# Expert results turned and shared out one step sooner, relational groups routed in pairs, and half of the values ahead of the scores

## The chip, the cores and the metric

The kernel runs on one core of one Trainium2 chip. The metric is the device time of one execution in microseconds (us). Five engines work side by side, each through its own list of instructions: TensorE (PE), VectorE (DVE), ScalarE (ACT), GpSimd (POOL) and SyncE (SP, whose part here is to issue transfers). They wait for one another by semaphores.

## The reference

The input x has 128 graphs of 64 nodes with 128 features, 8192 tokens in all. Four layers follow each other, each added to its input after a layer norm:

```
x = x + gnn0(layernorm(x), adj)       # 3 rounds: aggregate over adj, then a GRU cell
x = x + ffn0(layernorm(x))            # 8 experts, top 2 of 8 by gate score
x = x + gnn1(layernorm(x), nodemask, adj)   # relational graph conv
x = x + ffn1(layernorm(x))            # 8 experts, top 2, own layer norm, gelu

# an expert layer
scores = x @ Wg + bg;  top 2 experts of each token, weights p
h = relu(x @ W1[e] + b1[e])           # 128 -> 512   (gelu in the second)
y = h @ W2[e] + b2[e]                 # 512 -> 128
out = sum over the two experts of p[e] * y

# the relational layer, one direction
h = x @ W.T;  g = h @ Wg.T
vals = (h + b) * sigmoid(g + bg);  out = relu(sum over neighbours of vals)
```

## The kernel before, in words

Tokens lie in 64 tiles of 128, in 16 groups of four tiles. The stages follow one another: an opening (to about 106 us), the gated graph layer (to about 478), the first expert stage (to about 804), the relational layer (806 to 1066), the second expert stage (to about 1386) and the combine, which gathers each token's two results and writes the output. A value is kept as two 16-bit parts, hi and lo, so a product is three matmuls (the helper `passes`, L205 to L207). No scheduler is at work: every engine's order is the order of the calls in its own function, written by hand.

**An expert stage** (`experts`). Tokens have been sorted by expert into rows of the DRAM buffer `slots`, and are worked through in 36 blocks: 24 full blocks of 512 rows, and 12 blocks that are pairs of halves of 256 rows with an expert each. Buffers go round in rings of RING = 3. In its step b each engine does this:

- TensorE: for each quarter c of the hidden layer, `up_c(b + 1, c)` and `down_c(b, c)`, three matmuls each for a full block, twice as many of half the width for a pair. Then `turn(b - 1)`: four transposes (L1547) of the result that VectorE has put in `yT`, into the PSUM bank `YB`.
- ScalarE: for each quarter, the activation (L1586) and the hi part (L1592) of block b + 1.
- VectorE: `collect(b - 1)` (L1630), which takes the result of down out of PSUM, adds the bias and lets turn go; every third step `addresses` (L1617 to L1623), which works out rows and shares for three blocks; `share_out(b - 2)` (L1639), which multiplies the turned result by its tokens' weights; then four `lo` (L1605), the lo parts of block b + 1.
- GpSimd: four scatters (L1511) of block b to the DRAM buffer `results`, behind share_out.
- SyncE: the transposing load of block b + 3 (L1461), then the tags of block b + 2 (L1471), and in some steps a `tail` (L1477).

`rounds` writes the first steps out, puts a loop of six steps over the middle, and writes the last ones out.

**The relational stage** (`relational`). Group g passes through steps g to g + 4 and beyond. In step s TensorE turns group s - 1 (`turn_a`, L1861) and group s - 4 (`turn_b`, L1925), then computes the gate scores of group s - 4 (`scores`, L205 to L207 with WGATE and `xT_b`), the relational values of group s - 1 (`values`, four tiles in two PSUM halves v = 0 and 1; biases L1877, then products with WREL and `xT_a`) and the sums over neighbours of group s - 2 (L1890). A half of values waits until VectorE has taken the values before it out of the same PSUM half (`val_sb`).

VectorE's step: the mixture of the group's two expert results (L1674), lo parts, norms, values of group s - 2 (L2069, two halves), scores of group s - 4 (L2141, L2145), shifts (L2054 to L2064), `v_los` (L2091), and, when `chosen_at(s)` says so, the choice of two experts for one or two groups (L581 to L600, some lines further on the sorting). GpSimd computes the power for the norms (`root`, L1804) and sends finished rows of `ROWS` to `slots` by indirect transfers (L644); `relational_sends` says how many in which step. ScalarE turns PSUM copies into `xT_a` and `xT_b` (`turned_a`, `turned_b`, L2006) and, in the first SPLIT = 6 steps, scales by the norms itself (`norms_a`).

## Time and profile before

| what | value |
|---|---|
| median of 3 runs | 1425.64 us (1419.89 to 1427.88) |
| profiled execution, its own time | 1428.36 us |
| its span in the profile | 1426.6 us |
| mean granted TensorE clock, as a share of full speed | 0.787 |
| busy: PE / DVE / ACT / POOL | 918.1 / 905.9 / 765.8 / 733.9 us |

The span is what the profiler saw of the profiled execution; 1.76 us of that execution's time lie around it. Busy time counts an engine's own work and not its waits, branches or semaphores. A mean over the span mixes stages with different limits, so the stages are read one by one.

### The profile page before, as it was taken

To read this page: it belongs to the slowest core of one execution; us is meant where nothing else is said; L and a number is where in the kernel's file an instruction comes from. 1 tells how busy PE (TensorE), PEld (TensorE's weight loads), DVE (VectorE), ACT (ScalarE), POOL (GpSimd) and SP (SyncE) were. 2 spreads that over 40 slices of the span, in tenths; PEclk is the share of its full clock that TensorE was granted. 3 is DMA by queue.
4 is the path that set the end of the run, shared out by engine and by line. 5 is a ranking of instruction groups with operands and counts; after the bars stand their busy time and mean duration, and the time that the engine had idled before them with its cause. 6 is when DMAs were issued, how large, how long until landed. Compare 5 with 4: busy or idle time off the path is not lost. (4 is left out here: it accounts for less than half of the span.)

```text
span 1426.6 us, 23103 instructions
## 1 busy us (share of the span) xinstructions
PE 918.1 (64%) x5850; PEld 519.1 (36%) x5851; DVE 905.9 (64%) x2456; ACT 765.8 (54%) x1392; POOL 733.9 (51%) x717
## 2 busy tenths in 40 slices
PE   2368778888862357888787176656432968888820
PEld 1244344444432123434565133323210433346620
DVE  5967799999985345555544367767642645554626
ACT  2476767677762145666565165656431655666710
POOL 3501132876757646556544416567566444655540
PEclk9579999999995679899988555555556998999955
DMA  9233221221201524424221223321131342333209
GB/s 249 90 127 94 77 46 23 59 61 48 59 22 42 136 58 100 91 67 85 64 50 45 71 90 119 104 65 55 32 62 52 87 105 58 84 67 70 61 28 340
DMA packets 199164, 115.62 MB, mean 81 GB/s; under 512 B 155084, under 2 KB 175710, under 8 KB 198528
## 3 DMA queue, kind: packets, MB, share of 16 engines
q1 hardware_dynamic: 169008, 69.54, 20.8%
q0 software_dynamic: 17408, 34.13, 7.4%
q10 hardware_dynamic: 12624, 10.49, 2.8%
q8 instruction: 54, 0.88, 0.3%
q14 instruction: 70, 0.57, 0.1%
HBM read 43.80 MB, written 51.61 MB: 67 GB/s over the span
## 5 line engine op out<-in xcount | busy, mean ns | idle before, releaser
L644 POOL DMA_INDIRECT slots<-ROWS,pos x256 | 265.4, 1037 | 78.5 <-issue 71.4
L1511 POOL DMA_INDIRECT results<-e1ys,e1home x144 | 155.5, 1080 | 136.1 <-DVE e1ys L1639 93.7
L1511 POOL DMA_INDIRECT results<-e2ys,e2home x144 | 151.1, 1049 | 136.2 <-DVE e2ys L1639 93.0
L1586 ACT ACTIVATE e1hf<-psum,VT 128x512 f32<-128x512 f32 (+1 forms) x192 | 104.3, 583 | 151.6 <-PE psum L207 82.0
L1605 DVE SCALAR_TENSOR_TENSOR e1hs<-e1hf,e1hs 128x512 f16<-128x512 f32 x144 | 95.6, 690 | 127.4 <-ACT e1hs L1592 88.9
L1586 ACT ACTIVATE e2hf<-psum,VT 128x512 f32<-128x512 f32 (+1 forms) x192 | 104.8, 582 | 126.0 <-remote 59.1
L1605 DVE SCALAR_TENSOR_TENSOR e2hs<-e2hf,e2hs 128x512 f16<-128x512 f32 x144 | 95.8, 691 | 112.5 <-ACT e2hs L1592 83.0
L1363 POOL TENSOR_TENSOR a_Z<-a_Z,a_H 128x512 f32<-128x512 f32 x48 | 68.2, 1420 | 161.5 <-ACT a_Z L1093 159.2
L205 PE MATMUL psum<-e2hs,W 128*128 128x512 f16 (+1 forms) x192 | 66.7, 347 | 55.9 <-DVE e2hs L1605 25.9
L205 PE MATMUL psum<-a_hT,WHH 128*128 128x512 f16 x144 | 58.8, 408 | 52.5 <-ACT a_Z L1093 48.3
L205 PE MATMUL psum<-e1xT,W 128*128 128x512 f16 (+1 forms) x192 | 67.6, 352 | 38.5 <-DMA e1xT<-slots 16.7
L205 PE MATMUL psum<-e1hs,W 128*128 128x512 f16 (+1 forms) x192 | 67.4, 351 | 35.8 <-DVE e1hs L1605 24.9
L1592 ACT ACTIVATE e1hs<-e1hf 128x512 f16<-128x512 f32 x144 | 86.9, 631 | 0.0
L1592 ACT ACTIVATE e2hs<-e2hf 128x512 f16<-128x512 f32 x144 | 86.7, 631 | 0.0
L205 PE MATMUL psum<-e2xT,W 128*128 128x512 f16 (+1 forms) x192 | 66.7, 348 | 23.4 <-issue 11.0
L1804 POOL TENSOR_TENSOR c_rs<-c_var,mhalf 128x12 f32<-128x12 f32 (+2 forms) x22 | 40.5, 1843 | 79.9 <-DVE c_var L2082 45.1
L207 PE MATMUL psum<-e1xT,W 128*128 128x512 f16 (+1 forms) x192 | 67.7, 353 | 3.3 <-issue 3.2
L206 PE MATMUL psum<-e1hs,W 128*128 128x512 f16 (+1 forms) x192 | 67.5, 352 | 2.7 <-issue 1.7
L206 PE MATMUL psum<-e1xT,W 128*128 128x512 f16 (+1 forms) x192 | 67.5, 351 | 2.7 <-issue 2.7
L207 PE MATMUL psum<-e1hs,W 128*128 128x512 f16 (+1 forms) x192 | 67.4, 351 | 2.7 <-issue 2.5
L207 PE MATMUL psum<-e2xT,W 128*128 128x512 f16 (+1 forms) x192 | 66.5, 346 | 1.6 <-issue 1.5
L206 PE MATMUL psum<-e2xT,W 128*128 128x512 f16 (+1 forms) x192 | 66.5, 346 | 0.4 <-issue 0.4
(363 smaller groups left out, 2643.6 us busy)
## 6 DMA issues: line engine op xcount, KB each, us to landing
c_G<-results SPq DMA_DIRECT2D x32, 256.0 KB
d_G<-results SPq DMA_DIRECT2D x32, 256.0 KB, 5.2
slots<-slots SPq DMA_DIRECT2D x16, 264.0 KB
W<-in_L_ffn_W_dram SPq DMA_DIRECT2D x16, 256.0 KB, 3.4
kept<-a_cut SPq DMA_DIRECT2D x16, 256.0 KB, 2.6
slots<-ROWS,pos POOLq DMA_INDIRECT x256
W<-kept SPq DMA_DIRECT2D x8, 512.0 KB
out_dram<-X ACTq DMA_DIRECT2D x16, 256.0 KB, 7.1
```

The lines of the kernel that those rows point to most:

```text
L205: pe.matmul(out, lhs(0), rhs(0), start=start, stop=False, skip_group_check=True)
L206: pe.matmul(out, lhs(0), rhs(1), start=False, stop=False, skip_group_check=True)
L207: return pe.matmul(out, lhs(1), rhs(0), start=False, stop=stop, skip_group_check=True)
L644: pool.indirect_dma_start(out=slots, out_offset=bass.IndirectOffsetOnAxis(ap=k["pos"][:, c, t:t + 1], axis=0), in_=k["ROWS32"][:, t, :], i ...
L1363: pool.tensor_tensor(Z[p % 2][:, :], Z[p % 2][:, :], H[p][:, :], ALU.mult).then_inc(zh_sb, 1)
L1511: pool.indirect_dma_start(out=k["results"][m], out_offset=bass.IndirectOffsetOnAxis(ap=home[:, GT * b + q:GT * b + q + 1], axis=0), in_=ys ...
L1586: t = act.activation(hf[c][:, cols], HB[c][:, cols], func, bias=VT[:, bass.ds(e * CH + b1_col + c, 1)], scale=1 / PS)
L1592: act.activation(hs[j][:, 0, c, :], hf[c][:, :], ACT.Copy, scale=AS).then_inc(h_hi, 1)
L1605: dve.scalar_tensor_tensor(out=hs[j][:, 1, c, :], in0=hf[c][:, :], scalar=AS, in1=hs[j][:, 0, c, :], op0=ALU.mult, op1=ALU.subtract).then_ ...
L1804: pool.tensor_tensor(rstd[s % 4][:, lo:hi], var[s % 2][:, lo:hi], k["mhalf"][:, lo:hi], ALU.pow)\
```

## The change

The diff does three things. In the experts TensorE's turn of block b - 1 moves from the end of step b to behind its second quarter, VectorE shares out block b - 1 in step b instead of b - 2 (behind its second lo), the addresses are worked out one step earlier, and SyncE reads the tags ahead of the next load. In the relational stage the choice of experts is made for pairs of groups from the first on (the first two groups were chosen one by one), with the sends of GpSimd one step later and eight at once. And TensorE's values are split in two halves, the first of which stands ahead of the scores; ScalarE's `turned_b` stands ahead of `norms_a` where both are in a step.

```diff
--- before.py
+++ after.py
@@ -1488,6 +1488,8 @@
                     sp.wait_ge(counted, 1)
                 if RING <= b < RING + E:
                     tail(b - RING)
+                if 1 <= b and b + 2 < NBLK:
+                    read_tags(b + 2, rows.pop(b + 2))
                 if b + RING == EARLY:
                     sp.wait_ge(listed, 1)
                     sp.wait_ge(tails, 16 * E)
@@ -1495,8 +1497,6 @@
                 if b + RING < NBLK:
                     sp.wait_ge(h_ps, 4 * b + 4)
                     rows[b + RING] = load(b + RING)
-                if 1 <= b and b + 2 < NBLK:
-                    read_tags(b + 2, rows.pop(b + 2))
 
         @block.gpsimd
         def _(pool):
@@ -1568,8 +1568,8 @@
                         known[:] = [e, who(b + 2)]
                     elif c == 1:
                         known[:] = [e, None]
-                if not isinstance(b, int) or b:
-                    turn(b - 1, 1 - v)
+                    if c == 1 and (not isinstance(b, int) or b):
+                        turn(b - 1, 1 - v)
             rounds(pe, step)
             turn(NBLK - 1, (NBLK - 1) % 2)
 
@@ -1647,13 +1647,13 @@
             def step(b, j, i, v):
                 if not isinstance(b, int) or b:
                     collect(b - 1, 1 - v)
-                if j == RING - 1:
+                if j == 1:
                     addresses(b - j, i)
-                if not isinstance(b, int) or b > 1:
-                    share_out(b - 2, (j - 2) % RING, i - (j < 2), v)
                 for c in range(CH):
                     if not last(b):
                         lo(b + 1, (j + 1) % RING, c)
+                    if c == 1 and (not isinstance(b, int) or b):
+                        share_out(b - 1, (j - 1) % RING, i - (j < 1), 1 - v)
                 if m == 0 and isinstance(b, int) and b == RING - 1:
                     for h in range(2):
                         half = slice(h * NODES, (h + 1) * NODES)
@@ -1661,8 +1661,7 @@
             rounds(dve, step)
             end = NBLK - 1
             collect(end, end % 2)
-            for b in (end - 1, end):
-                share_out(b, b % RING, b // RING, b % 2)
+            share_out(end, end % RING, end // RING, end % 2)
 
 
 
@@ -1681,16 +1680,16 @@
         sp.dma_start(G[:, c, :, :], rows[:, c, bass.ds(GT * g, GT), :]).then_inc(sem, 16)
 
 
-BATCHES = [(0, 1), (1, 1)] + [(g, 2) for g in range(2, 16, 2)]
+BATCHES = [(g, 2) for g in range(0, 16, 2)]
 ROUTED = 4
 SPLIT = 6
 
 
 def relational_sends(NG):
 
-    first = ROUTED + 1
+    first = ROUTED + 2
     n = NG + ROUTED + 1
-    wanted = [0 if s < first else (8, 6, 2)[s - first] if s < first + 3 else 8 if s < NG else CARRY for s in range(n)]
+    wanted = [0 if s < first else 8 if s < NG else CARRY for s in range(n)]
     early = 2 * GT * (NG - QUAD)
     return [max(min(w, early - sum(wanted[0:s])), 0) for s, w in enumerate(wanted)]
 
@@ -1865,11 +1864,10 @@
                 pe.wait_ge(lo_a, g + 1)
                 turn_over(TAh, tok_a[p]).then_inc(a_ps, 1)
 
-            def values(g, p):
+            def values(g, p, v):
 
                 pe.wait_ge(a_sb, g + 1)
-                for q in range(GT):
-                    v = q // 2
+                for q in range(2 * v, 2 * v + 2):
                     if q % 2 == 0:
                         wait_from(pe, val_sb, 2 * g + v - 1)
                     o = Vv[v][:, q % 2, :, :].rearrange("p s d -> p (s d)")
@@ -1939,10 +1937,12 @@
                     turn_a(s - 1, (s - 1) % 2)
                 if 0 <= s - 4 < NG:
                     turn_b(s - 4)
+                if 0 <= s - 1 < NG:
+                    values(s - 1, (s - 1) % 2, 0)
                 if 0 <= s - 4 < NG:
                     scores(s - 4)
                 if 0 <= s - 1 < NG:
-                    values(s - 1, (s - 1) % 2)
+                    values(s - 1, (s - 1) % 2, 1)
                 if 0 <= s - 2 < NG:
                     neighbours(s - 2, s % 2)
                 b, g, n = chosen_at(s)
@@ -2008,10 +2008,10 @@
             def step(s):
                 if 0 <= s - 1 < NG:
                     turned_a(s - 1, (s - 1) % 2)
+                if 0 <= s - 4 < NG:
+                    turned_b(s - 4)
                 if s < SPLIT:
                     norms_a(s, s % 2)
-                if 0 <= s - 4 < NG:
-                    turned_b(s - 4)
                 if 0 <= s - 2 < NG:
                     v_his(s - 2, s % 2)
                 if SPLIT <= s < NG:
```

How the order of the instructions changes is shown at three places, with the line numbers of each version. The first is VectorE's list from collect on, for one full block in the first expert stage, without the last lo (e1yT is the collected result, e1ys the shared out one, e1hs the lo parts). Before:

```order
L1630 TENSOR_SCALAR e1yT<-psum,VT 128x512
L54 ISA
L1637 REGISTER_ALU
L1639 ISA
L1639 TENSOR_TENSOR e1ys<-psum,e1share 128x512
L1604 ISA
L1605 SCALAR_TENSOR_TENSOR e1hs<-e1hf,e1hs 128x512
L1604 REGISTER_ALU
L1605 SCALAR_TENSOR_TENSOR e1hs<-e1hf,e1hs 128x512
L1604 REGISTER_ALU
L1605 SCALAR_TENSOR_TENSOR e1hs<-e1hf,e1hs 128x512
```

After the change:

```order
L1630 TENSOR_SCALAR e1yT<-psum,VT 128x512
L1604 ISA
L1605 SCALAR_TENSOR_TENSOR e1hs<-e1hf,e1hs 128x512
L1604 REGISTER_ALU
L1605 SCALAR_TENSOR_TENSOR e1hs<-e1hf,e1hs 128x512
L54 ISA
L1637 REGISTER_ALU
L1639 ISA
L1639 TENSOR_TENSOR e1ys<-psum,e1share 128x512
L1604 REGISTER_ALU
L1605 SCALAR_TENSOR_TENSOR e1hs<-e1hf,e1hs 128x512
```

The sharing out moved from between collect and the four lo parts to behind the second of these, and it belongs to a block one later than it did.

The second place is TensorE's list in the last step of the first expert stage (e1hs times W are down's matmuls, e1yT turned by identf are the transposes). Before, the last down matmuls and what follows them:

```order
L205 REGISTER_ALU
L205 MATMUL psum<-e1hs,W 128x256
L206 MATMUL psum<-e1hs,W 128x256
L207 REGISTER_ALU
L207 MATMUL psum<-e1hs,W 128x256
L1547 MATMUL psum<-identf,e1yT 128x128 x8
L152 UNCONDITIONAL_BRANCH
```

After the change, the middle of the last block's matmuls:

```order
L205 REGISTER_ALU
L205 MATMUL psum<-e1hs,W 128x256
L206 MATMUL psum<-e1hs,W 128x256
L207 REGISTER_ALU
L207 MATMUL psum<-e1hs,W 128x256
L1547 MATMUL psum<-identf,e1yT 128x128 x4
L205 REGISTER_ALU
L205 MATMUL psum<-e1hs,W 128x256
```

Before, both the last two blocks' transposes stood at the very end (x8). Now those of the last but one stand behind half of the last block's matmuls, and four are left at the end.

The third place is TensorE's list in the fifth step of the relational stage (ident turns tokens and rows, WGATE are scores, relbias and WREL are values). Before, the dots standing for six more rows of scores in the same pattern:

```order
L1861 MATMUL psum<-ident,c_tok_a 128x128 x8
L1925 MATMUL psum<-ident,ROWS 128x128 x8
L205 MATMUL psum<-WGATE,c_xT_b 128x8
L206 MATMUL psum<-WGATE,c_xT_b 128x8
L207 MATMUL psum<-WGATE,c_xT_b 128x8
...
L205 MATMUL psum<-WGATE,c_xT_b 128x8
L206 MATMUL psum<-WGATE,c_xT_b 128x8
L207 MATMUL psum<-WGATE,c_xT_b 128x8
L1877 MATMUL psum<-relbias,ones 128x256 x2
L205 MATMUL psum<-WREL,c_xT_a 128x256
L206 MATMUL psum<-WREL,c_xT_a 128x256
L207 MATMUL psum<-WREL,c_xT_a 128x256
```

After the change:

```order
L1860 MATMUL psum<-ident,c_tok_a 128x128 x8
L1923 MATMUL psum<-ident,ROWS 128x128 x8
L1875 MATMUL psum<-relbias,ones 128x256 x2
L205 MATMUL psum<-WREL,c_xT_a 128x256
L206 MATMUL psum<-WREL,c_xT_a 128x256
L207 MATMUL psum<-WREL,c_xT_a 128x256
L1875 MATMUL psum<-relbias,ones 128x256 x2
L205 MATMUL psum<-WREL,c_xT_a 128x256
L206 MATMUL psum<-WREL,c_xT_a 128x256
L207 MATMUL psum<-WREL,c_xT_a 128x256
L205 MATMUL psum<-WGATE,c_xT_b 128x8
L206 MATMUL psum<-WGATE,c_xT_b 128x8
```

The scores' twelve matmuls moved behind the first two of the four tiles of values.

## Rows read from the trace of the kernel before

**Rows 1.** The page, part 1: busy us (share of the span) and instructions

```profile
PE 918.1 (64%) x5850; PEld 519.1 (36%) x5851; DVE 905.9 (64%) x2456; ACT 765.8 (54%) x1392; POOL 733.9 (51%) x717
```

**Rows 2.** Windows: stretch, length, busy per engine (instructions), granted clock, DMA share, GB/s

```profile
535.70:667.70 132.00, 110.84 (x505) 50.77 (x506) 76.48 (x135) 82.42 (x143) 76.62 (x72) 0.94 0.40 85
...
806.00:1066.00 260.00, 141.96 (x993) 77.56 (x994) 171.94 (x794) 134.07 (x276) 148.11 (x164) 0.51 0.26 79
1120.60:1252.30 131.70, 106.63 (x477) 48.11 (x476) 70.60 (x126) 80.14 (x139) 70.93 (x68) 0.91 0.36 83
```

**Rows 3.** Waits of ScalarE, 500 to 800 us: total, times, longest

```profile
ACT e1hf L1586 <- remote: 57.3, 13, 11.6
ACT e1hf L1586 <- PE psum L207: 54.2, 31, 8.8
```

**Rows 4.** Timeline of TensorE and VectorE: start, us, instruction, [idle before <-releaser]

```profile
566.20 0.38 PE L205 MATMUL psum<-e1hs,W 128*128 128x512 f16 x1 [2.88 <-DVE e1hs L1605]
...
566.78 0.63 PE L207 MATMUL psum<-e1hs,W 128*128 128x512 f16 x1
...
1156.60 0.60 PE L1547 MATMUL psum<-identf,e2yT 128*128 128x128 f32 x4
1157.04 0.38 PE L205 MATMUL psum<-e2xT,W 128*128 128x512 f16 x1
...
1159.62 0.38 PE L205 MATMUL psum<-e2xT,W 128*128 128x512 f16 x1
...
1162.21 0.60 PE L1547 MATMUL psum<-identf,e2yT 128*128 128x128 f32 x4
...
1158.91 0.75 DVE L1630 TENSOR_SCALAR e2yT<-psum,VT 128x512 f32<-128x512 f32 x1
...
1307.37 0.27 PE L205 MATMUL psum<-e2xT,W 128*128 128x256 f16 x1 [1.19 <-issue]
```

**Rows 5.** Timeline of GpSimd and VectorE at the expert stages' ends

```profile
789.11 0.98 POOL L1511 DMA_INDIRECT results<-e1ys,e1home  x1 [7.76 <-DVE e1ys L1639]
...
803.28 0.98 POOL L1511 DMA_INDIRECT results<-e1ys,e1home  x1 [0.30 <-issue]
...
1384.92 0.98 POOL L1511 DMA_INDIRECT results<-e2ys,e2home  x1 [0.31 <-issue]
...
780.51 0.69 DVE L1605 SCALAR_TENSOR_TENSOR e1hs<-e1hf,e1hs 128x512 f16<-128x512 f32 x1 [4.26 <-ACT e1hs L1592]
...
786.13 0.88 DVE L1630 TENSOR_SCALAR e1yT<-psum,VT 128x256 f32<-128x256 f32 x2 [0.69 <-issue]
...
787.65 0.69 DVE L1639 TENSOR_TENSOR e1ys<-psum,e1share 128x512 f32<-128x512 f32 x1
```

**Rows 6.** Timeline of VectorE in the relational stage, 847 to 855 us

```profile
847.71 0.74 DVE L2069 SCALAR_TENSOR_TENSOR c_sg<-psum,c_sg 128x256 f32<-128x256 f32 x2
...
850.97 0.18 DVE L581 TENSOR_REDUCE v_top<-S 128x4 f32<-128x32 f32 x1
...
853.50 0.19 DVE L600 TENSOR_TENSOR v_both<-v_wide 128x32 f16<-128x32 f32 x1
854.36 1.42 DVE L1674 TENSOR_TENSOR X<-X,c_G 128x512 f32<-128x512 f32 x2 [0.66 <-issue]
```

**Rows 7.** Timeline of TensorE at the same place

```profile
849.25 0.19 PE L205 MATMUL psum<-WGATE,c_xT_b 128*128 128x8 f16 x1 [2.56 <-ACT c_xT_b L2006]
...
849.66 0.60 PE L1877 MATMUL psum<-relbias,ones 1*128 1x256 f16 x2
...
852.24 0.60 PE L1877 MATMUL psum<-relbias,ones 1*128 1x256 f16 x2
```

**Rows 8.** Relational stage, VectorE, 868 to 1010 us: its waits, its score additions

```profile
DVE S L2141 <- PE psum L207: 15.9, 7, 3.3
DVE c_shift_a L2054 <- POOL c_rs L1804: 4.5, 3, 1.5
...
868.00:1010.00 142.00, 1.88 (x10) 0.51 0.26 80
```

## The prediction

> **What bounds the kernel now.** I began with the page's line of busy time [rows 1]: no engine passes 64% of the 1426.6 us, so no single engine is the bound. The stages were then set side by side by busy time in windows [rows 2]. The opening, the gated graph and the combine are untouched by the diff and are left out. What is left is the first expert stage, the relational stage (806 to 1066 us) and the second expert stage.
>
> The two expert stages run 24 full blocks and then 12 pairs of halves. Between their third and twenty-first turn lie 132.0 and 131.7 us, which is 18 steps of 7.33 us. TensorE works 107 to 111 us of each such stretch [rows 2], and where nothing disturbs it a step takes 5.62 us, from turn to turn [rows 4]. The difference is not spread evenly. The chain of waits of ScalarE [rows 3] puts 57.3 us in only 13 waits that nothing local ends, and 54.2 us in 31 waits for TensorE, the longest 8.8 us. What stops the loop for 3 to 8 us every few steps is not shown by a row that I found; a step between two stops is bound by TensorE.
>
> The relational stage is different. VectorE is busy 171.9 of 260.0 us and TensorE 142.0 at a granted clock of 0.51 [rows 2], the lower of its two levels (1.2 GHz). VectorE works through a fixed list, and its largest wait there is for the scores: 15.9 us in 7 waits over ten steps [rows 8]. So here VectorE's list, and what it waits for, is the time.
>
> **Part 1, the end of each expert stage: −9 us.** Before, block 33's products were scaled (share_out) only after the last step, so GpSimd stood idle 7.76 us and then issued twelve scatters in a row, from 789.11 to 803.28 + 0.98 [rows 5], 1.29 us each. Moved one step earlier, share_out(33) stands behind a lo of 780.51 [rows 5], and its four scatters fall into that idle time. Eight are left. Four scatters less are 4 × 1.29 = 5.1 us. They begin behind share_out(34), which needs collect(34), ended 786.13 + 0.88 = 787.01 [rows 5], a turn of 0.60 [rows 4] and a share of 0.69: about 788.3, against share_out(33)'s end at 787.65 + 0.69 = 788.34 now. So nearly nothing of the 5.1 is lost to the start. The turn now stands in front of half of the last block's down matmuls and holds them for about 1 us; block 35's scatters have four of 1.29 us in front of them as cover. I charge 0.5 us. The second expert stage ends with the same twelve, the last at 1384.92 [rows 5]. 2 × (5.1 − 0.5) = −9.2 us, and the relational stage and the combine wait for these ends.
>
> **Part 2, the middle of each expert step: 0, between −40 and +37 us.** VectorE's work is reordered and TensorE's four transposes move from a place where their input had long been ready to one where it is hardly ready. In the undisturbed step collect ends at 1158.91 + 0.75 = 1159.66, while the matmul in front of which the transposes now stand starts at 1159.62 [rows 4]: 0.04 us late. A second amount comes on top. Collect waits in VectorE's list for the last lo, and so for up's last piece of the step before. Between that piece and the place where collect is now needed, the transposes used to stand with 1157.04 − 1156.60 = 0.44 us [rows 4], and they don't any more. The loop from TensorE over ScalarE and VectorE back to TensorE so closes 0.04 + 0.44 = 0.48 us late, and the shortest step is 5.62 + 0.48 = 6.10 us. A step takes 7.33 on the mean, 1.2 us more than that; if the stops stay and take the wait into themselves, the price is 0. If each step pays it: 24 × 0.48 = 11.5 us, and for the 12 half blocks, whose collect takes 0.88 [rows 5], about 0.6 us each by the same loop, 7 us: 2 × 18.5 = 37 us over both experts. The other way, if a short wait in each step keeps the long stops from building up, a step could come down to some 6.5 us (0.4 above the shortest, my choice): 24 × 0.83 × 2 = −40 us. I take 0, since [rows 3] puts most of the loss in waits far longer than 0.48 us (57.3 / 13 = 4.4 us each in the first row). VectorE has the same instructions as before; the addresses come one step earlier behind tags that are read at the end of the step before, and the queue of SP waits for them once in three steps as it did. I cost both at nothing: loads are issued more than a step before use.
>
> The clock could make a wait dearer than its length. Behind an idle of 2.88 us the matmuls go from 0.38 to 0.63 us each [rows 4], the lower level of TensorE's clock. A wait of 1.19 us is followed by a matmul of half a block in 0.27 us [rows 4], which is the upper level. So a wait of 0.5 us should cost its own length. The Trainium skill ("TensorE: Matmul & The Clock Gate", section "Loop structure matters more than you think") says that the loop nest decides whether matmuls stay warm, and names a long wait between matmuls as the bad form. By that rule, if it held for the new waits, a step whose matmuls all ran at the lower level would pay 24 × 0.25 = 6 us on top of the wait; the trace shows such a fall only behind long stops, so the sum goes by the trace.
>
> **Part 3, pairs of groups in the relational stage: −2 us.** The first choice of experts for a single group falls away. It fills VectorE from 850.97 to 853.50 + 0.18 in the fifth step, and the next step's first instruction starts at 854.36 after 0.66 of issue [rows 6]: 2.7 us and some of the issue, −2.9 us. The choice for two groups at once then costs more than the one for a single group, since its operations grow from 32 to 64 columns (I choose a fifth, +0.5 us), and the placing moves one step behind: +0.2. GpSimd's first sends come one step later and eight at once; the same number is sent by the end, and its root of 2.30 us may be some 1 to 2 us later in one step, beside the choice. Sum −2.2 us, ends −3 and +1.
>
> **Part 4, values in front of scores: +10 us, between 0 and +15.** TensorE now computes the first half of values before the scores. In step 4 VectorE frees the first half of the values about 0.4 us after 847.71 [rows 6]; the scores' matmuls stood from 849.25, behind a wait of 2.56 us for ScalarE's turned copy [rows 7]. One half of values is 852.24 − 849.66 = 2.58 us at this clock [rows 7]. It fills TensorE's wait, but it cannot start before VectorE's own values, so the scores reach VectorE some 2.75 us behind these in every step, where VectorE has nothing else in its list. Ten steps of that are 27.5 us against the 15.9 it waits there now [rows 8]: +11.6, and for the 13 steps with this pattern +15. Three of the ten steps already lose 1.5 us waiting for GpSimd's root right behind [rows 8], 4.5 us that the later scores absorb: 15 − 4.5 = +10.5. The lower end, 0, is that waits elsewhere in the list (88 us of the stage are idle on VectorE, [rows 2]) take it all, or that a busier TensorE is granted its higher clock and the half takes 1.3 us. I take +10, near the rows. ScalarE's turned_b ahead of norms in two steps is nothing: the values are in front of its reader now.
>
> **Sum.** −9.2 + 0 − 2.2 + 10 = −1.4 us, on the profiled execution's own time of 1428.36: 1427.0 us. The median of the runs is 2.7 us under that execution, so 1424.3 in its terms; I say 1425.
>
> **The rivals.**
> - *Likeliest (0.45): the stops absorb the reordering.* 1418 to 1433, with −9 from the ends and about +8 from the scores.
> - *The turn becomes the bound (0.23).* Place: TensorE at the transposes in the middle of an expert step, held for collect. It decides from a quarter of its price on: 9 us turn "same" into slower; in full 37, or 1462. For it speaks that collect already ends 0.04 us after it will be needed [rows 4]. Against it, the 1.2 us that a mean step has above the shortest. This is the case on the slower side.
> - *A shorter loop (0.17).* Share_out one step sooner frees buffers and the long stops shrink: −10 to −40, so 1385 to 1415. For it, the 57.3 us of waits without a local cause [rows 3]; against it, the diff touches nothing that I can tie to them.
> - *The scores come no later (0.15).* The first half of values fits into TensorE's 2.56 us of wait [rows 7] and costs 0 to 3 us: 1415 to 1418.
> - *The waits in front of the turn cool TensorE (0.03, inside the 0.23).* Its matmuls then take 0.63 instead of 0.38 us for part of a step. Eight full steps of the 48 are enough for 8 × 6 = 48 us: 1473. Against it, the wait of 1.19 us that left the clock up [rows 4]. The Trainium skill's rule of the loop nest, cited above, speaks for this one.
>
> **How the numbers follow.** About 0.5% (7 us: below 1418.5, above 1432.8) is what a measurement of this kernel can tell from no change. Faster: 0.10 of the likeliest case, 0.15 of the shorter loop, 0.13 of the scores' case = 0.38. Slower: 0.08 + 0.20 = 0.28. Same: 0.34. The range of 8 in 10 reaches half into the two wide cases: 1403 to 1450; the likeliest case alone gives 1418 to 1433.
>
> **What would show it.** In the new profile: eight scatters behind each other at either expert's end, and GpSimd's idle time before them shorter; undisturbed expert steps of 6.1 instead of 5.62 us, with a short wait of TensorE for VectorE's collect in front of the transposes; the stretch of 18 steps still near 132 us; VectorE's wait for scores near 27 us in ten relational steps, and the stage near 266 us; no choice in its fifth step. The prediction is wrong if the long stops of the expert loop change in number or length, since I could name no cause for them, or if the waits for scores don't grow.

## The result and the profile after

The changed kernel took 1442.62 us in the median of 17 runs (1431.73 to 1447.49), the kernel before beside it 1430.11 us (1409.90 to 1453.73): a ratio of 1.0128, with a 95% interval of 1.0091 to 1.0164, so the change is slower. The ratio leaves out the executions of the kernel before that took over 1.5% longer than its fastest; the two medians as they stand give 1.0087. The profiled execution took 1443.63 us with a span of 1441.5, 14.9 us more than before's.

The windows of the changed kernel (columns as in [rows 2]) show where these lie. The first two are the 18 steps between the third and twenty-first turn of either expert stage, the last reaches from the first mixture of the relational stage to the first product of the second experts:

```profile
540.80:670.60 129.80, 110.51 (x505) 50.24 (x505) 74.73 (x132) 84.68 (x144) 78.23 (x71) 0.97 0.37 85
1140.50:1270.50 130.00, 110.17 (x504) 50.28 (x504) 74.32 (x132) 83.52 (x142) 79.18 (x73) 0.96 0.39 88
807.40:1080.10 272.70, 139.28 (x985) 78.40 (x986) 168.34 (x774) 132.29 (x272) 142.51 (x123) 0.50 0.23 70
```

and the same relational stretch of the kernel before:

```profile
810.10:1063.00 252.90, 138.96 (x986) 76.49 (x987) 171.01 (x793) 132.64 (x274) 144.76 (x122) 0.51 0.25 77
```

In the first expert stage 18 steps are 2.2 us shorter than before. For the second stage the row of [rows 2] can't be used: it has 477 matmuls where 18 steps have 505, so it covers 17 steps. All 18 of the kernel before lie in

```profile
1120.60:1258.20 137.60, 112.48 (x506) 50.90 (x505) 75.62 (x134) 85.09 (x147) 74.91 (x72) 0.91 0.37 84
```

which is 7.6 us more than after the change. The relational stretch is 19.8 us longer, with hardly more work in it (0.3 us on TensorE, 1.9 on its weight loads, less on the others): it is waiting. All that lies outside it gives back 4.9 us, 2.7 ahead of it and 2.2 behind it, which makes the 14.9. VectorE's score additions say which wait it is. These are the changed kernel's, all 16 of the stage, with the idle time in front of them:

```profile
L2141 DVE TENSOR_TENSOR S<-psum,c_rs x16: 181/192/193, 848.5 to 1069.0; 128x32 f32<-128x32 f32 x16
...
  PE psum L207: 42.3, 15
```

and these the kernel before's:

```profile
L2141 DVE TENSOR_TENSOR S<-psum,c_rs x16: 179/191/192, 849.8 to 1052.4; 128x32 f32<-128x32 f32 x16
...
  PE psum L207: 21.7, 11
```

20.6 us more in this one wait. Within a step of the changed kernel (timeline of VectorE, then TensorE; ten of the 13 steps have this wait of 2.77 us, three a longer one) one sees the chain:

```profile
906.20 0.75 DVE L2069 SCALAR_TENSOR_TENSOR c_sg<-psum,c_sg 128x256 f32<-128x256 f32 x2
909.72 0.19 DVE L2141 TENSOR_TENSOR S<-psum,c_rs 128x32 f32<-128x32 f32 x1 [2.77 <-PE psum L207]
...
906.77 0.58 PE L1875 MATMUL psum<-relbias,ones 1*128 1x256 f16 x2 [1.58 <-DVE c_sg L2069]
...
909.18 0.21 PE L205 MATMUL psum<-WGATE,c_xT_b 128*128 128x8 f16 x1
```

VectorE frees the first half of the values, TensorE has idled 1.58 us for that, computes 2.4 us of values at the lower clock, then the scores; VectorE stands still for 2.77 us.

At the end of the first expert stage the scatters look so (timeline of GpSimd, then of VectorE; ten scatters of the same pitch lie between the first two rows):

```profile
784.97 1.33 POOL L1511 DMA_INDIRECT results<-e1ys,e1home  x1 [4.24 <-DVE e1ys L1639]
...
799.48 0.98 POOL L1511 DMA_INDIRECT results<-e1ys,e1home  x1 [0.30 <-issue]
...
783.51 0.68 DVE L1639 TENSOR_TENSOR e1ys<-psum,e1share 128x512 f32<-128x512 f32 x1
...
786.13 0.88 DVE L1630 TENSOR_SCALAR e1yT<-psum,VT 128x256 f32<-128x256 f32 x2 [0.68 <-issue]
```

There are still twelve scatters in a row, but they begin ahead of the collect of block 34 (786.13) and not behind it. From the start of that collect to the end of the last scatter it is 14.3 us; before, it was 18.1 (786.13 to 804.26, [rows 5]). In the second stage it is 13.1 us instead of 18.1. So the two ends are 3.8 and 5.0 us shorter, and all the rest outside the relational stretch is 3.9 us longer in these two executions.

The long stops of the expert loop changed their form. ScalarE's waits from 500 to 800 us that nothing local ends were 13 with 57.3 us [rows 3]; they are now fewer, while its waits for TensorE grew from 54.2 to 71.3:

```profile
ACT e1hf L1586 <- PE psum L207: 71.3, 46, 7.0
ACT e1hf L1586 <- remote: 24.0, 4, 10.1
```

### The profile page after: what moved, and what is told of

The parts are those of the page before. It is cut to its first block and busy times, and to the rows that moved or that the text cites. A ratio compares the mean times of both kernels' runs of the same rounds, so it can differ in the third digit from the quotient of the medians.

```text
span 1441.5 us, 23094 instructions
## 1 busy us (share of the span) xinstructions
PE 915.9 (64%) x5849; PEld 523.1 (36%) x5850; DVE 902.1 (63%) x2437; ACT 768.9 (53%) x1390; POOL 739.9 (51%) x717
## 3 DMA queue, kind: packets, MB, share of 16 engines
q0 software_dynamic: 17408, 34.13, 7.3%
## 5 line engine op out<-in xcount | busy, mean ns | idle before, releaser
L1511 POOL DMA_INDIRECT results<-e1ys,e1home x144 | 158.7, 1102 | 129.2 <-DVE e1ys L1639 87.3
L1511 POOL DMA_INDIRECT results<-e2ys,e2home x144 | 155.6, 1081 | 130.3 <-DVE e2ys L1639 87.8
L205 PE MATMUL psum<-e1hs,W 128*128 128x512 f16 (+1 forms) x192 | 66.2, 345 | 10.3 <-DVE e1hs L1605 9.8
L207 PE MATMUL psum<-e1hs,W 128*128 128x512 f16 (+1 forms) x192 | 65.5, 341 | 0.7 <-issue 0.7
L206 PE MATMUL psum<-e1hs,W 128*128 128x512 f16 (+1 forms) x192 | 65.8, 343 | 0.0
```

The lines of the kernel that those rows point to most:

```text
L205: pe.matmul(out, lhs(0), rhs(0), start=start, stop=False, skip_group_check=True)
L206: pe.matmul(out, lhs(0), rhs(1), start=False, stop=False, skip_group_check=True)
L207: return pe.matmul(out, lhs(1), rhs(0), start=False, stop=stop, skip_group_check=True)
L1511: pool.indirect_dma_start(out=k["results"][m], out_offset=bass.IndirectOffsetOnAxis(ap=home[:, GT * b + q:GT * b + q + 1], axis=0), in_=ys ...
```

## The experiments

Each kernel was timed in rounds with the kernel before on the same chip. **The chips differ.** On the chip of the first four, the kernel before took 1227.7 us; on the others 1418 to 1432 us. A ratio therefore only speaks for its kind of chip.

**The parts alone, on the chip where the kernel before takes 1227.7 us.** First, the changed kernel with the split undone:

```diff
+                if 0 <= s - 4 < NG:
+                    scores(s - 4)
                 if 0 <= s - 1 < NG:
                     values(s - 1, (s - 1) % 2, 0)
-                if 0 <= s - 4 < NG:
-                    scores(s - 4)
-                if 0 <= s - 1 < NG:
                     values(s - 1, (s - 1) % 2, 1)
```

> The changed kernel with one part undone: TensorE computes the scores ahead of both halves of the values again; experts, pairs and ScalarE's order stay changed. Theory 1 (the first half of the values keeps VectorE waiting for the scores): the stretch from the first to the last mixture of the relational stage falls from 200.9 us to 183 or less (before: 183.3), VectorE's waits for the scores in the steps 4 to 16 fall from 39 to about 19 us, and the kernel takes about 18 us less than the changed one: near 1.000 of the kernel before, or 0.5% under it if the shorter ends of the experts count. Theory 2 (the later and larger sends and choices of the pairs cost the time): the stretch stays near 200 us and the ratio near 1.013.

Second, the reverse, the kernel before with only that split:

> The kernel before with one part alone: the first half of the values ahead of the scores on TensorE. Theory 1: the relational stage grows by 18 to 21 us, ratio 1.013 to 1.015. Theory 2: by 0 to 5 us, ratio under 1.004. The expert stages are those of before.

Third, the kernel before with only the expert part (SyncE's, TensorE's and VectorE's edits of `experts` in the diff above):

> The kernel before with the expert part alone (turn, share out, addresses and tags one step sooner). By the profiles, each expert stage ends with 8 scatters in a row instead of 12, and the steps in the middle cost nothing on balance: ratio 0.994 to 1.000. If the turn in the middle of the step is a bound that the one profile hid, ratio 1.005 to 1.02, with undisturbed steps of 6.1 us instead of 5.62.

Fourth, only BATCHES and `relational_sends`:

> The kernel before with the pairs alone (choices for two groups from the first on, sends from step 6 on, eight at once). Theory 1: one choice less, minus 2 to 3 us from the first to the last mixture, ratio 0.997 to 1.000. Theory 2: the stretch grows by 5 us or more.

| run | ratio | interval | relational stretch, us | wait for scores, us |
|---|---|---|---|---|
| r1_no_split | 1.0434 | 1.0419 to 1.0448 | 235.4 | 3.3 |
| r2_split_only | 1.0120 | 1.0101 to 1.0139 | 250.4 | 39.3 |
| r3_experts_only | 1.0437 | 1.0420 to 1.0455 | 236.4 | 5.8 |
| r4_pairs_only | 1.0002 | 0.9990 to 1.0014 | 235.6 | 6.3 |

Theory 1 holds in kind: the split alone makes the relational stretch 14.0 us longer than with the experts' part alone (250.4 against 236.4), and it alone brings the wait for the scores. The cost is less than the 18 to 21 us expected, because another wait shrinks: 33.5 us more are spent on the scores than in r3 (39.3 against 5.8), and the wait for GpSimd's root right behind them falls from 20.5 to 3.9 us. These are VectorE's waits for the root in r3 and then in r2:

```profile
DVE c_shift_a L2053 <- POOL c_rs L1803: 20.5, 13, 3.2
```

```profile
DVE c_shift_a L2055 <- POOL c_rs L1804: 3.9, 4, 1.2
```

The pairs are worth nothing that can be measured; theory 2 falls. But the expert part, which looked free in the profile after, costs 54 us here. The windows of 18 expert steps, r4 and then r3:

```profile
511.80:613.00 101.20, 101.20 (x505) 50.67 (x505) 77.83 (x135) 85.39 (x142) 79.13 (x72) 1.00 0.55 112
```

```profile
511.40:627.10 115.70, 107.39 (x505) 49.88 (x505) 74.34 (x132) 85.27 (x144) 85.61 (x76) 0.98 0.44 98
```

Without the expert part a full step takes 5.62 us all the time: here the fastest step of [rows 4] is the only one, and TensorE is never idle in this window. With it, the mean is 6.43 us: most steps take 6.20 from turn to turn, a few up to 8.6. The half blocks behind them pay more, 7.05 us a step against 5.68 in most steps of r4. The ends are shorter here too: from the collect of block 34 to the end of the last scatter 14.4 and 14.3 us in r3, 18.9 and 19.5 in r4. So the middle of the steps costs the 54 us and the 9.7 that the ends give back, some 64 us. The waits of TensorE in the window, its timeline in r3, then VectorE's and two rows of ScalarE's:

```profile
PE psum L1547 <- DVE e1yT L1630: 12.7, 19, 5.0
```

```profile
551.64 0.65 PE L1547 MATMUL psum<-identf,e1yT 128*128 128x128 f32 x4 [0.55 <-DVE e1yT L1630]
...
557.96 0.66 PE L1547 MATMUL psum<-identf,e1yT 128*128 128x128 f32 x4 [0.49 <-DVE e1yT L1630]
...
555.00 0.68 DVE L1639 TENSOR_TENSOR e1ys<-psum,e1share 128x512 f32<-128x512 f32 x1
555.61 1.29 DVE L1605 SCALAR_TENSOR_TENSOR e1hs<-e1hf,e1hs 128x512 f16<-128x512 f32 x2
557.16 0.75 DVE L1630 TENSOR_SCALAR e1yT<-psum,VT 128x512 f32<-128x512 f32 x1 [0.25 <-issue]
...
554.37 0.69 ACT L1586 ACTIVATE e1hf<-psum,VT 128x512 f32<-128x512 f32 x1
554.96 1.14 ACT L1592 ACTIVATE e1hs<-e1hf 128x512 f16<-128x512 f32 x2
```

TensorE waits at every turn for collect, and collect stands behind the last two lo parts. The share_out of 555.00 in front of these delays them little: the last lo needs ScalarE's last hi part, which ends at 554.96 + 1.14 = 556.10, and it takes 0.69 us itself, so it could not end before 556.79; it ends at 555.61 + 1.29 = 556.90. In a half block the same wait is longer, and 0.68 us of issue stand in front of collect (r3, TensorE, then VectorE):

```profile
660.11 0.66 PE L1547 MATMUL psum<-identf,e1yT 128*128 128x128 f32 x4 [1.15 <-DVE e1yT L1630]
...
659.18 0.88 DVE L1630 TENSOR_SCALAR e1yT<-psum,VT 128x256 f32<-128x256 f32 x2 [0.68 <-issue]
```

**The expert part in variants, where the kernel before takes 1431 us.** The changed kernel again; the expert part alone with the turn and share_out at `c == 2` instead of `c == 1`; with the turn at `c == 1` and share_out at `c == 3`; and the kernel before with the pairs, with addresses and tags one step sooner as in the change, and with turn and share_out moved in the last step only (`if c == 1 and last(b)`):

```diff
-                    if c == 1 and (not isinstance(b, int) or b):
+                    if c == 2 and (not isinstance(b, int) or b):
                         turn(b - 1, 1 - v)
...
-                    if c == 1 and (not isinstance(b, int) or b):
+                    if c == 2 and (not isinstance(b, int) or b):
                         share_out(b - 1, (j - 1) % RING, i - (j < 1), 1 - v)
```

(the first variant, against the expert part of the change; the second has `c == 3` in the second place only; the third, against the kernel before, TensorE's part of it:)

```diff
+                    if c == 1 and last(b):
+                        turn(b - 1, 1 - v)
-                if not isinstance(b, int) or b:
+                if (not isinstance(b, int) or b) and not last(b):
                     turn(b - 1, 1 - v)
```

> The changed kernel itself, again beside the kernel before. If the chip is like that of the first experiments (expert steps of 5.6 us without long stops in the kernel before, which took 1227.7 us there), the experts' part costs 52 to 55 us and the values' part 14 to 16 us, and the ratio is 1.053 to 1.057. If it is like that of the first measurement (1430 us for the kernel before, long stops), the ratio is 1.010 to 1.016.

> The expert part alone, but turn and share_out stand behind the third quarter (c == 2) instead of the second. Theory A (TensorE is held at turn for collect, which comes too late there): a quarter later collect is 1.3 us early, TensorE no longer waits, the steps come back to 5.6 to 5.8 us and the ratio is 0.99 to 1.005. Theory B (VectorE's share_out between the lo parts holds ScalarE and with it the next products): the ratio stays at 1.03 or above.

> The expert part alone, the turn behind the second quarter as in the change, but share_out behind the last lo part instead of the second. Theory A: collect is even later by 0.69 us, since it stands behind share_out, and the ratio rises above 1.044, to some 1.06. Theory B: ScalarE is freed and the ratio falls to 1.01 to 1.02.

> The kernel before with the pairs and, of the expert part, only its end: addresses and tags one step sooner as in the change, but turn and share_out move only in the last step, so that the steps in the middle keep their order. If the shorter end is worth what the trace says and the middle is what costs, the ratio is 0.992 to 0.998; if the moved tags or addresses cost something, 1.002 or above.

| run | ratio | interval | 18 steps in its profile, us |
|---|---|---|---|
| s3_changed | 1.0098 | 1.0062 to 1.0133 | 130.7 |
| s1_turn_later | 1.0174 | 1.0119 to 1.0229 | 143.0 |
| s2_share_last | 1.0042 | 1.0004 to 1.0080 | 122.9 |
| s6_tail_pairs | 1.0010 | 0.9920 to 1.0099 | 143.0 |

The kernel before spread from 1399 to 1456 us beside these four, so small differences between the ratios mean little; the plain medians give 1.0061, 1.0061, 0.9991 and 0.9958. Theories A and B had been made for a chip without stops and say little here: 18 steps take 123 to 143 us against the 101 of the other chip, whatever the order. Neither is borne out: A expected s1 below 1.005 and s2 at 1.06, B had s1 at 1.03. None of these orders was run on a chip without stops, so what each would be worth there stays open. The shorter end alone (s6) can't be told from no change; it had been expected at 0.992 to 0.998.

**What the stops are.** Next the expert part alone on this kind of chip; the kernel before without one matmul in three (the second line of `passes` left out for the experts' two products); VectorE's order changed (v_los and shifts, then scores, then the choice); and the last with the pairs and the shorter end:

```diff
     pe.matmul(out, lhs(0), rhs(0), start=start, stop=False, skip_group_check=True)
-    pe.matmul(out, lhs(0), rhs(1), start=False, stop=False, skip_group_check=True)
     return pe.matmul(out, lhs(1), rhs(0), start=False, stop=stop, skip_group_check=True)
```

```diff
+                if 0 <= s - 2 < NG:
+                    v_los(s - 2, s % 2)
+                if SPLIT <= s < NG:
+                    shifts_a(s, s % 2)
+                if 0 <= s - 3 < NG:
+                    shifts_c(s - 3, (s - 3) % 2)
                 if 0 <= s - 4 < NG:
                     scores(s - 4)
-                if s >= SPLIT:
-                    choose(s)
...
+                choose(s)
```

> The expert part alone, again. On a chip on which the kernel before takes about 1430 us and its expert steps have long stops: if the stops come from TensorE itself being held after dense work (theory C), the waits for collect replace part of them, the 18 steps stay at 128 to 134 us and the ratio is 0.992 to 1.004. If the stops come from elsewhere and simply add (theory D), the ratio is 1.03 or above, as on the chip where the kernel before took 1227.7 us. On a chip without stops both say 1.044.

> The kernel before, which leaves out one of the three matmuls of each product in both expert layers (hi times lo), so TensorE has 16 matmuls of 0.22 us in a step instead of 24 and the step is set by ScalarE at about 5.0 us. Where the kernel before has long stops: theory C says that a TensorE with a third less to do is hardly held, so that 18 steps fall from 132 us to 90 to 100 and the kernel by 5% or more; theory D says that the stops stay, at 115 to 125 us for 18 steps. Where it has none, 18 steps go from 101 to about 90 us, ratio 0.97 to 0.98.

> The kernel before with VectorE's order alone changed in the relational stage: v_los and the shifts stand ahead of the scores, the choice last, so that this work lies inside the wait for the scores. Theory 1 (VectorE's list with its wait for the scores sets the stage) says that 0.7 to 1.4 us are hidden in each of 13 steps: the stage 8 to 15 us shorter, ratio 0.990 to 0.995. If something else sets the step, for instance ScalarE or GpSimd's root, the stage moves by less than 3 us.

> The kernel before with three changes: the pairs, the expert stage's end alone (turn and share_out moved only in the last step), and VectorE's v_los and shifts ahead of the scores. By the theories so far minus 2, minus 4 to 9 and minus 8 to 15 us: ratio 0.983 to 0.992.

Measured: t2 0.9959 (0.9909 to 1.0010), t3 0.9882 (0.9763 to 1.0000), t1 1.0151 (1.0034 to 1.0268), t4 0.9969 (0.9900 to 1.0037). So the expert part, 4.4% on the first chip, costs nothing here that can be measured. Theory C, that TensorE is held for its own density, falls with t3: with a third of the matmuls gone the kernel is 1.2% faster and not 5%, and in its profile 18 steps take as long as before:

```profile
533.90:667.40 133.50, 93.82 (x361) 40.02 (x362) 75.05 (x134) 80.64 (x141) 76.85 (x72) 0.80 0.38 84
```

VectorE's new order (t1) took the wait for the scores away and nothing was won in the stage, since the waits only moved. Its relational stretch, 823.5 to 1077.7 us, is 254.2 us long against 252.9. Most of the 1.5% by which the kernel is slower lies elsewhere: in its profile the stage begins 13 us later than before, behind stages that the edit doesn't touch, and why is open. Both t1 (expected at 0.990 to 0.995) and t4 (0.983 to 0.992) missed. VectorE's waits in that stretch:

```profile
DVE c_vs L2091 <- ACT c_vs L1989: 27.4, 16, 4.6
DVE c_shift_a L2054 <- POOL c_rs L1804: 10.2, 11, 3.3
...
DVE S L2141 <- PE psum L207: 2.7, 1, 2.7
```

A look back at the kernel before shows the shape of a stop. Timeline of TensorE and ScalarE, and a window inside it:

```profile
1138.64 0.38 PE L207 MATMUL psum<-e2xT,W 128*128 128x512 f16 x1
...
1142.96 0.38 PE L207 MATMUL psum<-e2xT,W 128*128 128x512 f16 x1
1150.65 0.58 PE L205 MATMUL psum<-e2hs,W 128*128 128x512 f16 x1 [7.31 <-DVE e2hs L1605]
...
1140.34 0.69 ACT L1586 ACTIVATE e2hf<-psum,VT 128x512 f32<-128x512 f32 x1 [2.49 <-PE psum L207]
1148.59 0.69 ACT L1586 ACTIVATE e2hf<-psum,VT 128x512 f32<-128x512 f32 x1 [7.56 <-remote]
...
1143.40:1148.40 5.00, 0.00 (x0) 0.00 (x0) 0.00 (x0) 0.00 (x0) 2.94 (x3) 0.83 0.48 119
```

ScalarE's list puts the first two activations of a block next to each other; these are the two above. The second needs the third matmul of up's second quarter, which is the one of 1138.64, and from VectorE only a lo part of the block before. It starts 9.95 us after that matmul, though TensorE's records go on at full pace until 1142.96. In the window TensorE, VectorE and ScalarE stand, and of the engines GpSimd alone goes on, with scatters. That suggested the next two: plain transfers to fixed places instead of the scatters (112 rows each, with four more at the stage's end for the rows that are left), and no transposing loads after the third block; beside them the relational parts once more, with both halves of the values ahead of the scores (`values(…, 0)`, `values(…, 1)`, then `scores`).

```diff
-                    pool.indirect_dma_start(
-                        out=k["results"][m],
...
+                    pool.dma_start(k["results"][m][448 * b + 112 * q:448 * b + 112 * q + 112, :],
+                                   ys[b % RING][0:112, q * P:(q + 1) * P]).then_inc(y_stored[b % RING], 16)
```

```diff
+                    if b < RING:
                         sp.dma_start_transpose(turned_rows(b, b % RING, h), x_rows[bass.ds(row, n), 0:2 * P])\
                             .then_inc(x_loaded[b % RING], 16)
+                    else:
+                        sp.dma_start(turned_rows(b, b % RING, h)[0:1, 0, 0:128], x_rows[bass.ds(row, 1), 0:P])\
+                            .then_inc(x_loaded[b % RING], 16)
```

> The kernel before, which leaves out the scattering of the experts' results: GpSimd stores each block's rows by four plain transfers of 112 rows to fixed places instead of four indirect ones of 128 (the combine then adds wrong rows). Where the kernel before has long stops in the experts: if GpSimd's indirect transfers bring them about (theory S), 18 steps fall from 132 us to about 105 and the kernel gets 4 to 8% faster, beyond the some 20 us that shorter ends of the stages give. If the chip or other transfers do, the 18 steps stay at 125 us or more. On a chip without stops the steps stay at 5.6 us.

> The kernel before, which leaves out the transposing loads of the experts' blocks from the fourth on: one row is fetched instead, so each block computes with old rows. If the transposing loads bring about the long stops (theory L), 18 steps fall from 132 us to about 105; otherwise they stay at 125 us or more. On a chip without stops they stay at 5.6 us.

> The changed kernel without the split of the values, again. On a chip with long stops (kernel before about 1430 us) the expert part alone gave 0.996 and the pairs 1.000, so this gives 0.992 to 0.999, against about 1.010 to 1.013 for the changed kernel; on a chip without stops 1.043 as before.

> The changed kernel with both halves of the values ahead of the scores on TensorE, instead of one. If each half of 2.6 us goes straight onto VectorE's wait for the scores, in each of 13 steps another 2.6 us are added: the stretch from the first to the last mixture grows from 201 us to 225 to 235 and the ratio to the kernel before by another 0.018 to 0.024 over that of the changed kernel. If the time of the change has another source in the relational stage, the stretch grows by less than 10 us.

The plain stores took 1278.43 us, 0.8962 (0.8889 to 0.9034) of the kernel before, and their 18 steps are those of the first chip (about 11 of the 154 us won lie behind the last turns of the two expert stages):

```profile
537.60:638.80 101.20, 101.20 (x505) 50.66 (x506) 76.88 (x135) 85.45 (x142) 39.02 (x76) 1.00 0.52 105
```

Without loads the median is 1434.52 us against 1432.29 (its profile has 18 steps of 137.3 us). Theory S holds, theory L falls: on this kind of chip the long stops in the experts come with GpSimd's indirect stores. The plain stores go through the same software queue, with 17,664 packets and 34.11 MB in the whole kernel against 17,408 and 34.13 before (u1, then before), so it is neither the bytes nor the number of packets on it:

```profile
q0 software_dynamic: 17664, 34.11, 8.8%
```

```profile
q0 software_dynamic: 17408, 34.13, 7.4%
```

What is left is the indirection, the scattered places, or GpSimd's own work for a store (its busy time in 18 steps falls from 76.62 to 39.02 us); no run tells these apart. With the split undone (u3) the ratio is 0.9993 (0.9953 to 1.0034); with both halves first (u4) 1.0204 (1.0138 to 1.0270). Relational stretches of u3 and u4:

```profile
809.00:1065.80 256.80, 139.35 (x984) 76.32 (x984) 169.03 (x774) 132.71 (x272) 144.81 (x123) 0.51 0.24 75
```

```profile
809.70:1097.90 288.20, 141.67 (x984) 76.94 (x984) 168.46 (x774) 131.83 (x272) 141.95 (x122) 0.50 0.22 67
```

No half, one half and two halves in front of the scores give 256.8, 272.7 (268.6 in s3's profile) and 288.2 us: 12 to 16 us for the first half and 16 to 20 for the second, or 0.9 to 1.5 us in each of 13 steps, not the 2.6 that a half lasts. Against the other profiles of this kind of chip with the scores first and the indirect stores in place (before, s1, s2, s6, t2: 250.5 to 253.7 us) the first half costs up to 22 us. The expectation of 225 us or more from the first to the last mixture is missed (it is 215.9), and so is that of the ratio, which rises by 0.008 to 0.011 over that of the changed kernel and not by 0.018 to 0.024; that half after half costs the stage more is borne out.

Last, the expert part on top of the plain stores, against these alone:

> The expert part of the change on top of plain stores, which leave out the scattering of results (four plain transfers of 112 rows to fixed places) and with it the long stops. If the stops only covered the cost of the expert part, it now appears: 18 steps of 6.3 to 6.5 us (113 to 117 us) instead of 101.2, and a ratio to the kernel before about 0.035 above that of the plain stores alone. If the expert part is free in itself, the two are equal within 0.005.

> The plain stores alone again, on the same chip as the run with the expert part: 18 steps of 101 to 102 us, whichever chip it is.

1335.71 us (1333.05 to 1343.61) against 1271.42 (1268.37 to 1279.35), ratios of 0.9552 and 0.9073. The windows of 18 steps, v1 and v2:

```profile
542.40:658.30 115.90, 108.23 (x504) 50.02 (x504) 74.26 (x132) 85.03 (x144) 37.24 (x72) 0.97 0.41 90
```

```profile
539.00:640.30 101.30, 101.28 (x504) 50.50 (x505) 76.88 (x135) 85.41 (x142) 38.99 (x75) 1.00 0.51 105
```

So the cost of the expert part is there on this kind of chip too, 64 us, as soon as the stops are gone, as much as the middle of the steps costs on the first chip. It is more than expected (0.048 in the ratio instead of about 0.035). Under the stops it is hidden.

## Why the prediction was right or wrong

**Part 4 is the step that failed, by its size.** The mechanism was right, place and length of the wait too (2.75 us forecast, 2.77 in ten of the 13 steps). The term was +10 us, at most +15. The stretch grew by 19.8 us between the two profiles, by 12 to 22 over all profiles of this kind of chip, and by 14.0 on the first chip. Forecast for the wait itself was +15 in 13 steps; it grew by 20.6. Of the difference, 3.1 us are three steps that waited 3.40, 3.83 and 4.13 us instead of 2.77; in the kernel before the same three had waited 1.76, 3.25 and 2.57, and the profiles don't show why they are longer. Another 2.3 us come from taking ten steps' mean of the old wait, 1.59 us, for all 13, which had 1.42. And the 4.5 us that the wait for the root was to absorb came back only in part: the root's waits of 8.4 us in the stage shrank to 4.8, while the waits for ScalarE's relu part grew from 0.8 to 4.8. The lower bound of 0, VectorE's other idle time taking it all, had nothing behind it in any run.

**Part 3 was too hopeful by 2 us.** The choice is gone from the fifth step, but r4 gives 1.0002 (0.9990 to 1.0014) for −2.2 us forecast.

**Part 1 was right in its sum, not in its picture.** Minus 4.6 us were forecast for an end; measured are −3.8 and −5.0, and −4.5 and −5.2 between r4 and r3. Eight scatters in a row were to show it, and they did not come: share_out(33) came at 783.51 and not soon after 780.51, so that its four scatters stand directly in front of the eight. They begin early enough all the same.

**Part 2, forecast 0 between −40 and +37, was near 0 on the kind of chip of the measurement and +64 on the other.** On the first kind, the ratios 0.9959 (t2) and 0.9993 (u3) say so, and the two profiles give +3.9 us for all that is neither an end nor the relational stretch. The likeliest case, that the stops absorb it, is what t2, v1 and v2 show together. The price of the rival was too small. For a full step the loop was nearly right: 6.10 us forecast, 6.20 in most steps, but 6.43 in the mean. For a half block 0.6 us were charged and 1.37 measured (7.05 against 5.68); the 0.69 us of issue in front of its collect [rows 5] are not in the sum and would fill most of the gap, which is argued and not tested. The mean step was misread as well: 7.33 us hold for the first stage, but the second stage's 131.7 us are 17 steps of 7.75. The prediction had named a change in the stops as a sign that it is wrong, and that sign came (13 waits without a local releaser before, 4 after), though the stage's length hardly moved. The sentence that the stops' cause is shown by no row was true; an experiment on the engine that alone goes on within a stop would have found where they come from. The Trainium skill's rule of the loop nest ("TensorE: Matmul & The Clock Gate", section "Loop structure matters more than you think"), which the prediction weighs there, did not decide anything. In v1, with a wait at every turn, TensorE's granted clock is 0.97 in its window above, and in r3 a wait of 0.49 us goes with a step that is 0.58 us longer (6.20 against 5.62): such short waits cost about their length.

**The sum.** Forecast 1425 us, range 1403 to 1450; measured 1442.6. The forecast was no change on balance, with 0.28 for slower. That the measured time lies within the range is luck: the width comes from Part 2, and the time was lost in Part 4. By the two profiles the ends give −8.8 (−9.2 forecast), the relational stretch +19.8 (+7.8 forecast, Parts 3 and 4) and the rest +3.9 (0 forecast): +14.9 instead of −1.4. The kernel before's median on the day of the measurement also stood 4.5 us above the one I started from.

## What to carry to other kernels

Moving work in front of a semaphore that an engine with a fixed list waits for can cost time in every iteration, even if it fills a gap of the engine that does it: put the short product that others wait for first. Here 2.4 us of work moved in front cost 1.1 to 1.5 us in each of 13 steps. It is less than its length where it takes the place of another wait, so count both: on one chip 33.5 us more of one wait took 16.6 us off the next.

An edit that looks free under long stops should be read again without them: the same edit cost 4.4% where the stops were absent and 5% where an experiment had taken them away. When engines stand still together, look at which one goes on. And count the instructions in a window before it is divided into steps: equal stretches should hold equal numbers.

## What the hardware showed that was not expected

The same kernel took 1227.7 us on one chip and 1418 to 1432 us on others, with the same instructions. On the others ScalarE at times starts some 10 us after the matmul that it needs (1138.64 to 1148.59 in the kernel before), and its long waits of this kind, 13 without a local releaser and 31 for TensorE, sum up to 111.5 us in 300 [rows 3]. Replacing the 288 indirect stores of the experts by plain ones issued by the same engine (u1, 4 × 112 rows a block) removes 154 us and every such stop in the 18 steps. The Trainium skill ("DMA: Bandwidth & Descriptors", section "SWDGE vs HWDGE vs iDMA") says that GpSimd builds the descriptors of its transfers in software and writes them into rings in the on-chip memory. The plain stores of u1 go through the same software queue, so this alone does not tell the stores that bring the stops from those that don't. No run here shows in which way an indirect store holds up TensorE's signals, nor why one chip is free of it; both stay open.
